# Summing expert heads on GpSimd instead of VectorE, with a third buffer of masked products

## What is computed

```python
q = (hidden @ Wq).reshape(b, t, 2, H, 64)                    # H = 4 heads
sim = einsum('btphn,hkpn->pbthk', q, keys)                   # 64 + 64 keys
sc, ix = top_k(sim, 8)
all_sc = sx[..., :, None] + sy[..., None, :]                 # 64 candidates
scores, pk = top_k(all_sc, 8)                                # 8 of 1024 experts
w = silu(einsum('btd,bthkd->bthk', hidden, down_embed[idx])) * softmax(scores)
experts = einsum('bthk,bthkd->btd', w, up_embed[idx])
mlp = silu(hidden @ Wg + bg) * (hidden @ Wu + bu) @ Wd + bd
return mlp + experts
```

## Time and profile before

| | |
|---|---|
| median of 3 runs | 2605.49 us |
| the profiled execution, its own time | 2603.14 us |
| its span, first to last instruction | 2601.4 us |
| TensorE busy | 89% |
| VectorE busy | 74% |
| ScalarE busy | 40% |
| GpSimd busy | 3% (83.3 us) |
| mean granted TensorE clock, of full speed | 0.978 |

### The profile page before, as it was taken

One profiled execution on the slowest core, in us unless ns is written; L12 is line 12 of the kernel. 1 busy time (PEld: TensorE's weight loads), 2 busy tenths in 40 slices (PEclk: granted clock), 3 DMA queues, 4 the chain that ended last, 5 costly groups with the idle time before them and its releaser, 6 DMA issues. The chain is left out here.

```text
span 2601.4 us, 37919 instructions
## 1 busy us (share of the span) xinstructions
PE 2310.9 (89%) x12768; PEld 1602.4 (62%) x12768; DVE 1923.2 (74%) x5516; ACT 1042.0 (40%) x1350; POOL 83.3 (3%) x135
## 2 busy tenths in 40 slices
PE   5888888889999899899987998898999989989998
PEld 4666665667667667667654454444766766766765
DVE  4655556467988888988984555555798888898897
ACT  1112222224454354444335555555445435434433
POOL 3200000000000000000000000000000000000000
PEclk9999999999999999999998999999999999999999
DMA  6000000000000000000000000000000000000000
GB/s 195 1 1 0 0 0 0 0 0 1 1 0 1 1 0 1 1 0 1 1 1 1 1 1 1 0 0 1 1 9 0 9 9 0 9 9 0 8 9 9
DMA packets 20769, 18.13 MB, mean 7 GB/s; under 512 B 6556, under 2 KB 19872, under 8 KB 20649
## 3 DMA queue, kind: packets, MB, share of 16 engines
q1 hardware_dynamic: 16106, 14.04, 1.8%
q10 hardware_dynamic: 4542, 2.78, 0.4%
HBM read 12.60 MB, written 4.19 MB: 6 GB/s over the span
## 5 line engine op out<-in xcount | busy, mean ns | idle before, releaser
L1272 ACT ACTIVATE f_E<-f_two 128x1024 f32<-128x1024 f32 x256 | 248.1, 1021 | 324.3 <-PE f_two L1154 324.3
L1008 DVE SCALAR_TENSOR_TENSOR f_E<-f_two,f_E 128x1024 f32<-128x1024 f32 x256 | 312.4, 1220 | 70.1 <-ACT f_E L1272 61.2
L1144 PE MATMUL f_acc<-ue,f_mid 128*128 128x256 f32 x1024 | 254.1, 394 | 12.1 <-DVE f_mid L993 12.0
L1144 PEld LDWEIGHTS f_acc<-ue,f_mid 128*128 128x128 f32 x1024 | 191.9, 194 | 55.4 <-DVE f_mid L993 19.4
L1059 PE MATMUL f_two<-f_hT,wg 128*128 128x512 f32 x768 | 211.4, 410 | 9.6 <-DVE f_mid L877 9.6
L1059 PE MATMUL f_two<-f_hT,wu 128*128 128x512 f32 x768 | 199.9, 395 | 0.0
L1242 ACT ACTIVATE f_gate<-f_two,bg 128x512 f32<-128x512 f32 x128 | 88.1, 688 | 270.0 <-PE f_two L1059 269.6
L1101 PE MATMUL f_acc<-wd,f_mid 128*128 128x256 f32 x768 | 188.1, 388 | 0.0
L1720 ACT ACTIVATE b_U<-b_two 128x768 f32<-128x768 f32 (+1 forms) x192 | 160.7, 886 | 65.4 <-PE b_two L1590 65.4
L1059 PE MATMUL f_two<-f_hT,deT 128*128 128x512 f32 x768 | 184.3, 395 | 0.0
L622 PE MATMUL zb<-wz,a_wave 128*128 128x256 f32 x576 | 179.9, 403 | 4.8 <-ACT a_wave L693 4.8
(11 more groups left out here) (252 smaller groups left out, 3980.4 us busy)
## 6 DMA issues: line engine op xcount, KB each, us to landing
x<-in_L_attn_a_x SPq DMA_DIRECT2D x8, 512.0 KB, 7.5
out_x<-x SPq DMA_DIRECT2D x8, 512.0 KB, 2.9
de_rows<-in_L_ffn_down_embed ACTq DMA_DIRECT2D x1, 1024.0 KB, 6.0
wd<-in_L_ffn_Wd SPq DMA_DIRECT2D x1, 1024.0 KB, 9.9
ue<-in_L_ffn_up_embed SPq DMA_DIRECT2D x16, 64.0 KB, 5.3
whole_g<-in_L_ffn_Wg SPq DMA_DIRECT2D x1, 1024.0 KB, 5.2
whole_u<-in_L_ffn_Wu SPq DMA_DIRECT2D x1, 1024.0 KB, 8.7
ffq<-in_L_ffn_Wq ACTq DMA_DIRECT2D x4, 128.0 KB, 9.2
```

What stands on the lines that cost most here:

```text
L1008: dve.scalar_tensor_tensor(out=two_heads, in0=wide(turns, ("R", u))[:], scalar=PICKED_ABOVE, in1=two_heads, op0=ALU.is_gt, op1=ALU.mult).t ...
L1144: mm = pe.matmul(acc[:, j * C:(j + 1) * C], mixed[c % 2][:, j * P:(j + 1) * P], w.ue[:, c, :], start=False, stop=True, skip_group_check=True)
L1272: act.activation(E[:, c % 2, 2 * p:2 * p + 2].rearrange("p h t -> p (h t)"), wide(turns, ("S", u))[:], ACT.Exp).then_inc(S.act_read, 1)
```

## The change

GpSimd does `add_heads` for chunks 0 to 5 of each round (`POOL_SUMS = 6`), VectorE keeps chunks 6 and 7. `E` gets a third buffer, `E_third`, and chunk c uses buffer c % 3; ScalarE waits for the sum of chunk c - 3 before it writes chunk c. VectorE's sums signal a semaphore of their own, `late_added`. `ffn_deviations` moves behind GpSimd's sum of chunk 0 (before, it stood alone), and so do the deviations of the next layer in the last round.

```diff
+        E, E_third = tmp("E", [P, 2, H, T]), tmp("E_third", [P, H, T])
+        chunk_E = [E[:, 0], E[:, 1], E_third[:]]
+        POOL_SUMS = FC - 2
...
                     def mix(c):
                         both = pairs[c % 2]
-                        dve.wait_ge(S.heads_added, i * FC + c + 1 + START)
+                        if c < POOL_SUMS:
+                            dve.wait_ge(S.heads_added, i * POOL_SUMS + c + 1 + START)
+                        else:
+                            dve.wait_ge(S.late_added, i * (FC - POOL_SUMS) + c - POOL_SUMS + 1 + START)
...
-                        if p == 0 and c >= 1:
+                        if p == 0 and c > POOL_SUMS:
                             add_heads(c - 1)
...
             def _(pool):
                 def a_round(i, turns, last):
-                    for c in range(FC):
-                        if c == 3 and not last:
+                    for c in range(POOL_SUMS):
+                        pool.wait_ge(*turns.dve_has_read(i, ("R", 2 * c + 1)))
+                        if c == 1:
+                            pool.wait_ge(S.mid_used, i * FC + FC + START)
+                        if c >= 2:
+                            pool.wait_ge(S.mix_ready, i * FC + c - 1 + START)
+                        pool.tensor_tensor(pairs[c % 2], chunk_E[c % 3][:, 0:2], chunk_E[c % 3][:, 2:4], ALU.add
+                                           ).then_inc(S.heads_added, 1)
+                        if c == 0 and not last:
                             ffn_deviations(pool, w, S, i + 1)
+                        if c == 0 and last and tag == "f1":
+                            attn_deviations(pool, w, 0)
...
-                        if c >= 2 and p == 0:
-                            act.wait_ge(S.heads_added, i * FC + c - 1 + START)
+                        if c >= 3 and p == 0:
+                            act.wait_ge(S.heads_added, i * POOL_SUMS + c - 2 + START)
```

More of the change, by code:

```diff
@@ L75, in __init__ @@
             "dve_read sim_half sim_first rank_step below_ready expo_ready total_ready ln_ready digits_ready "
-            "lo_scores shifted heads_added mix_step mix_ready mix_used mid_used x_added "
+            "lo_scores shifted heads_added late_added mix_step mix_ready mix_used mid_used x_added "
         ).split()]
@@ L80, in __init__ @@
          self.sim_first, self.rank_step, self.below_ready, self.expo_ready, self.total_ready,
-         self.ln_ready, self.digits_ready, self.lo_scores, self.shifted, self.heads_added, self.mix_step,
+         self.ln_ready, self.digits_ready, self.lo_scores, self.shifted, self.heads_added, self.late_added, self.mix_step,
          self.mix_ready, self.mix_used, self.mid_used, self.x_added) = self.all
@@ L728, in experts_ffn @@
         hot_x = xn[:].rearrange("p j c -> p (j c)").bitcast(BF16).rearrange("p (g r i) -> p g r i", g=G, i=KPH)
-        E = tmp("E", [P, 2, H, T])
+        E, E_third = tmp("E", [P, 2, H, T]), tmp("E_third", [P, H, T])
+        chunk_E = [E[:, 0], E[:, 1], E_third[:]]
+        POOL_SUMS = FC - 2
         mid = tmp("mid", [P, 4, T])
@@ L997, in add_heads @@
                         dve.wait_ge(*turns.dve_has_read(i, ("R", 2 * c + 1)))
[L998 to L1001, removed]
+                        dve.tensor_tensor(pairs[c % 2], chunk_E[c % 3][:, 0:2], chunk_E[c % 3][:, 2:4], ALU.add
+                                          ).then_inc(S.late_added, 1)
                     for u in range(UNITS):
                         c, p = u // 2, u % 2
-                        two_heads = E[:, c % 2, 2 * p:2 * p + 2].rearrange("p h t -> p (h t)")
+                        two_heads = chunk_E[c % 3][:, 2 * p:2 * p + 2].rearrange("p h t -> p (h t)")
                         dve.wait_ge(*turns.act_has_read(i, ("S", u)))
@@ L1010, in a_round @@
                         if u == UNITS - 2:
-                            last_rows = E[96:P, c % 2, 0]
+                            last_rows = chunk_E[c % 3][96:P, 0]
                             dve.wait_ge(*turns.filled(i, ("o", 0)))
@@ L1043, in _ @@
                 a_round(ROUNDS - 1, final, last=True)
-                if tag == "f1":
-                    attn_deviations(pool, w, 0)
             @block.tensor
@@ L1269, in a_round @@
                         act.wait_ge(*turns.filled(i, ("S", u)))
-                        if c >= 2 and p == 0:
-                            act.wait_ge(S.heads_added, i * FC + c - 1 + START)
-                        act.activation(E[:, c % 2, 2 * p:2 * p + 2].rearrange("p h t -> p (h t)"),
+                        if c >= 3 and p == 0:
+                            act.wait_ge(S.heads_added, i * POOL_SUMS + c - 2 + START)
+                        act.activation(chunk_E[c % 3][:, 2 * p:2 * p + 2].rearrange("p h t -> p (h t)"),
                                        wide(turns, ("S", u))[:], ACT.Exp).then_inc(S.act_read, 1)
```

## The result

The changed kernel takes 2687.53 us (median of 4 runs, 2680.57 to 2694.65) against 2604.07 us in the same comparison: 3.3% slower, ratio 1.0325 (95% interval 1.0286 to 1.0364). Forecast: 2684 us, slower with a chance of 0.83. The profiled execution took 2694.65 us, its span 2692.7.

The account below looks back on a forecast made before the run. In the sparse part VectorE's 4.86 us per chunk bounds, against a 4.58 us TensorE/ScalarE chain; TensorE paces the dense part. Holds of 16 x 4.9 = 78.4 us on 2603.14, plus 2.35, give 2684 us; range 2615 to 2708.

Parts of the forecast that it names:

- VectorE held for nearly the whole sum: Main case, chance 0.79: mix's second half stands until GpSimd's 2.37 us sum is nearly through; own range 2650 to 2708 us.
- order of events: Step-by-step round: GpSimd's sum enters between mix's halves, next mask starts at m+4.85, 6.0 us per chunk instead of 4.86.
- Chunk 2's double loss: Sum 1, then sum 2's length, pass before mix(1) is done at 664.9; mask(3,0) comes 1.8 us late.
- Mask(4,0) and mask(5,0): Mask starts after chunks 3 and 4, forecast at 670.85 and 678.6: 3.0 and 4.1 us late.
- Chunks 5 to 7: Mix(4) delays chunk 4's expert product; mask(7,0) and similarities come 4.9 us late, nothing further lost in chunks 6 and 7.
- Total: 16 rounds x 4.9 us = 78.4 us lost, giving 2684 us.
- Rival 1: VectorE isn't held, GpSimd waits or fits in behind: 16 us won, 2589 us; chance 0.14.
- threshold of 0.85 us: Hold length above which VectorE's chunk (3.73 us without the sum) exceeds the 4.58 us chain of TensorE and ScalarE.
- Rival 2: Short hold: VectorE stands 1.2 us, its chunk is 4.93 us, kernel between 2603 and 2640 us; chance 0.07.
- The signs: Expected profile: L998 at 0.69 or about 2.9 us, mean above 1.5; expert products of chunks 1 to 4 wait for L998.
- forecast 98.6: Expected spacing in us at which GpSimd's first deviation recurs, instead of 93.7.

Follow-up runs that it names:

- one input: Changed kernel with both halves of mix on VectorE made reductions with one SBUF input, adding of halves and product with reach left out: 2588.71 us, ratio 0.9924.
- half the length: Changed kernel with GpSimd's sums cut to 128x512, the second half left out, released at the same moments: 2596.99 us, ratio 0.9971.
- spread fills: Changed kernel plus small groups of zero-weight matmuls in TensorE's longer waits in chunks 3 to 6: 2672.65 us, ratio 1.0253.
- kernel with three sums: Changed kernel with GpSimd summing only chunks 0 to 2, VectorE 3 to 7, three buffers kept: 2648.77 us, ratio 1.0160.
- late-sum kernel: Changed kernel with one wait changed: GpSimd starts the sum of chunk c (from 1) only when mix(c-1) is done: 2595.27 us, ratio 0.9964.

## Why the prediction was right

The mechanism and its place came out as forecast. The total did too, but in part by luck: the holds cost less than I had, and the clock, which I had put at nothing, made up for it.

- *VectorE held for nearly the whole sum:* right, and shown from three sides (another moment, one input, half the length). GpSimd gets in between the halves of mix, as in the order of events. The hold is 1.96 us where I had 2.3: the sum has 2.2 us left when VectorE lets go, since a part of its start runs before, and the product ends 0.55 behind it and not 0.7. So the next mask comes at m+4.5, not m+4.85.
- *Chunk 2's double loss:* right in place, smaller. From the first score fill, mask(3,0) came at 18.75 us (663.28 - 644.53) against 17.23 before (663.03 - 645.80): 1.5 late, forecast 1.8. Sum 2 won the race against the first half of mix(1), which I had left open.
- *Mask(4,0) and mask(5,0):* 2.3 and 3.3 us late (24.37 and 31.98 us behind the first fill, before 22.09 and 28.67), forecast 3.0 and 4.1. The shortfall is the shorter hold, once per chunk.
- *Chunks 5 to 7:* I had 0.8 more and 4.9 at the end. The similarities came 5.2 late, 1.9 more. Most of the difference is the clock: a term that the prediction didn't have. It had noted 1.00 in the earlier trace rows and a fall nowhere. Without it, as the spread fills show, this round would have lost 3.6 us. My path is the one at full clock: in the spread kernel the product at 682.18 waits 1.21 us for mix(4), while in the changed kernel the same product (683.67) stands behind an R fill that waits for the exp of scores that came late at half clock.
- *Total:* 83.5 us measured, 78.4 forecast, but as 16 x 4.9 of holds. It was about 16 x 3.6 = 58 of holds, so I had these 1.3 us too high in each round. In the profiled execution the expert layers lost 78.0 us, so some 20 of them are the clock's (26 by the first round's share), and layer "b" added 14.6. How much of the 83.5 between the medians lies in "b" is open, since only one execution was profiled. That 2684 lies within 4 us of 2687.5 is luck.
- *Rival 1's price:* 16 us. Its situation was made twice: 2588.7 with one input, ratio 0.9924 (20 us), 2595.3 with the sum behind mix, ratio 0.9964 (9 us). In "f1" a round at full clock took 1.2 us less in its sparse part (38.24 against 39.4), which would be 19 us in 16 rounds; in the second kernel the falls of the clock in half of the rounds took part of that back. Its threshold of 0.85 us fits too: at a hold of 0.88 the kernel was not slower than before.
- *Rival 2* (a hold of 1.2 us): not the case, the hold was 1.96 us. A hold of 1.2 us was never made.
- *The signs:* L998's mean over its 128 is 1.44 us, (107.7 + 76.5) / 128, where I had above 1.5, since mix(1) was held in its first half and the others at 2.65 to 2.73 us and not 2.9. Of the expert products of chunks 1 to 4 only the first waits for L998 in the round shown (1.24 us, at 663.42); the others stand behind work of TensorE that waits longer.
- One row was misread: the 93.73 in the earlier trace rows is GpSimd's idle time, not its period, which was 94.2 to 96.6 us in "f1" (95.2 to 95.4 in the steady rounds without a fall) and 99.3 to 101.1 after. The forecast 98.6 stood on the wrong base, and the growth of a round, 4.9 us in the mean, was as forecast; nothing else rested on it.

## What to carry to other kernels

Before giving an elementwise operation to GpSimd, look at what VectorE does while it runs, not only at how long it takes: if both have two inputs in SBUF, the second stood here until the first was as good as through, and two VectorE operations linked by a semaphore leave a gap in which GpSimd gets in. The cure was one wait: start the sum behind the pair of operations that it would hold, and 3.3% lost became 0.4% won. Look at the kind of the operation too: masks and the turned input, with one input in PSUM, ran beside the sum without loss. And price a wait on TensorE twice, once for its length and once for the work behind it at half clock.

## What the runs showed that I had not expected

- The clock's part. Falls of TensorE's granted clock came with its waits: 0.72 over the 12 us with a wait of 3.31 us in them, and a product of 1.93 us at 3.71 behind it. In the kernel with three sums the fall began inside a wait of 1.24 us, and in the late-sum kernel seven of 14 rounds have one in a sparse part whose longest waits are 1.0 us. The kernel before has falls too (114 us in all). Where the next fall lands changes with small shifts of the queue: filling one wait moved it to another place and cost 25 us, filling four saved 15 us.
- GpSimd's sum and VectorE run side by side without loss when VectorE's operation is a reduction with one SBUF input (0.69 and 2.35 us), or a mask or TENSOR_TENSOR with its other input in PSUM (1.22 and 2.34 to 2.36 us).
- A GpSimd sum of 128x512 took 1.27 us at its fastest, of 128x1024 2.33 to 2.36; held by VectorE's first half of mix they are recorded at 1.56 and 2.64. A recorded span includes the time in which the operation stood.
